# Causal mask of a chunked state-space scan: from mask matmuls to a GpSimd select

## What is computed

```python
def step(state, inp):
    x_t, b_t, c_t, dt_t = inp
    decay = jnp.exp(dt_t * a)[..., None, None]      # a < 0, 8 heads
    b_bar = dt_t[..., None] * b_t
    state = decay * state + b_bar[..., None] * x_t[:, :, None, :]
    y_t = jnp.einsum('bhn,bhnp->bhp', c_t, state)
    return (state, y_t)
```

## Time and profile before

| | |
|---|---|
| median of 3 runs | 1684.99 us (1682.63 to 1688.21) |
| the profiled execution's own time | 1682.11 us |
| its span in the trace | 1680.3 us |
| mean granted TensorE clock | 0.941 of full |
| TensorE busy | 1496.8 us, 89% |
| VectorE busy | 1211.4 us, 72% |
| ScalarE busy | 662.6 us, 39% |
| GpSimd busy | 473.3 us, 28% |

### The profile page before, as it was taken

The page is one execution under the profiler, slowest core; times in us unless marked ns, Lnnn a source line. Parts: engine busy times, 40 slices in busy tenths (PEclk is TensorE's granted clock), DMA queues, the critical chain, the costliest instruction groups (busy, mean ns, idle before and its releaser), DMA issues.

```text
span 1680.3 us, 22635 instructions
## 1 busy us (share of the span) xinstructions
PE 1496.8 (89%) x8504; PEld 924.9 (55%) x8504; DVE 1211.4 (72%) x2746; ACT 662.6 (39%) x1193; POOL 473.3 (28%) x496
## 2 busy tenths in 40 slices
PE   7989979998999979999899989999899998997445
PEld 2436635665456645666356654666456663565334
DVE  1357897489775897578974897858974789747861
ACT  4451434533263332714346332643337143551012
POOL 3003431336103341043313261043410443122610
PEclk9999999999999989999899989999899998999756
DMA  7000010011002010020100110020100201001100
GB/s 270 1 0 26 7 44 16 15 53 44 22 1 67 1 50 17 1 67 7 44 17 10 58 45 22 1 67 7 44 16 1 67 7 44 16 5 38 44 22 4
DMA packets 47309, 54.25 MB, mean 32 GB/s; under 512 B 7384, under 2 KB 42072, under 8 KB 47200
## 3 DMA queue, kind: packets, MB, share of 16 engines
q1 hardware_dynamic: 41184, 46.45, 8.4%
q0 software_dynamic: 6016, 6.35, 1.4%
HBM read 34.86 MB, written 17.87 MB: 31 GB/s over the span
## 4 chain that ended last, share of the span: by engine, by line
PE 38%; issue 27%; DVE 20%; POOL 9%; ACT 3%; DMA 2%; DVEq 0%; POOLq 0%
PE ps L1450 18%; PE ps L1602 7%; DVE xT L951 5%; POOL EC L519 4%; DVE Mt L1182 3%; PE ps L1515 2%; PE ps L1509 2%; DMA Mt<-mask,midx 2%; PE ps L1554 1%; POOL out L594 1%; ACT BT L637 1%; DVE st L889 1%; DVE EC L1173 1%; PE ps L1635 1%; PE ps L1438 1%
## 5 line engine op out<-in xcount | busy, mean ns | idle before, releaser
L1450 PE MATMUL ps<-xT,wb_s 128*128 128x512 f32 x512 | 232.0, 600 | 8.9 <-ACT xT L676 8.9
L1450 PE MATMUL ps<-xT,wc_s 128*128 128x512 f32 x512 | 237.7, 615 | 0.0
L726 ACT ACTIVATE Eg<-ps 128x512 f32<-128x512 f32 x128 | 76.4, 597 | 295.8 <-DVE Mt L1046 219.7
L951 DVE SCALAR_TENSOR_TENSOR xT<-xc,cols_s,xT 128x512 f32<-128x512 f32 x192 | 162.5, 892 | 3.2 <-ACT xT L669 0.6
L1450 PEld LDWEIGHTS ps<-xT,wc_s 128*128 128x128 f32 x512 | 99.4, 198 | 115.3 <-issue 114.9
L1450 PEld LDWEIGHTS ps<-xT,wb_s 128*128 128x128 f32 x512 | 94.3, 191 | 119.5 <-issue 103.9
L1450 PE MATMUL ps<-hT,wz_s 128*128 128x512 f32 x256 | 122.4, 635 | 0.0
L1602 PE MATMUL ps<-CT,xT 128*128 128x256 f32 x512 | 113.3, 382 | 7.7 <-DVE xT L1134 7.7
L587 POOL TENSOR_TENSOR sm<-sm,mhalf 128x1 f32<-128x1 f32 x24 | 14.5, 604 | 374.5 <-DVE sm L1337 345.0
L1450 PE MATMUL ps<-hT,wx_s 128*128 128x512 f32 x256 | 114.7, 603 | 0.9 <-ACT hT L648 0.9
L1602 PEld LDWEIGHTS ps<-CT,xT 128*128 128x128 f32 x512 | 98.2, 192 | 24.3 <-issue 11.1
(11 more groups left out here) (286 smaller groups left out, 3017.8 us busy)
## 6 DMA issues: line engine op xcount, KB each, us to landing
BT<-x SPq DMA_DIRECT2D x8, 1024.0 KB, 5.4
xr<-x SPq DMA_DIRECT2D x8, 1024.0 KB, 7.2
x_scratch<-xr SPq DMA_DIRECT2D x32, 256.0 KB, 2.5
out<-EC SPq DMA_DIRECT2D x32, 256.0 KB, 2.2
modrow<-mod_scratch SPq DMA_DIRECT2D x8, 512.0 KB, 4.0
w_s<-w SPq DMA_DIRECT2D x2, 1024.0 KB, 11.7
xT<-wmod SPq DMA_DIRECT2D x1, 1024.0 KB, 8.7
wb_s<-wbT SPq DMA_DIRECT2D x1, 1024.0 KB, 11.1
```

The source lines that it names most:

```text
L726: a.activation(Eg[:, s * HALF:(s + 1) * HALF], ps[s][:, :], ACT.Exp).then_inc(Eg_ready, 1)
L951: ins = v.scalar_tensor_tensor(dst, xcv[:, m, half * HALF + tap:half * HALF + tap + HALF], cols_s[:, m, tap:tap + 1], dst, ALU.mult, ALU.add)
L1450: ins = t_.matmul(bank[:, :], w[:, k, m * P:(m + 1) * P], rhs[:, k, half * HALF:(half + 1) * HALF], start=k == 0, stop=k == nk - 1)
```

## The change

The two mask matmuls of a chunk go, and the tile `causal` with them. The decay difference is then not masked, and above the diagonal it is positive. So ScalarE makes two passes for each half: Relu of minus the difference from PSUM into `Eg`, which bounds the exponent at zero, then the exponential of minus that in place. GpSimd then sets the entries with t < s to zero, in place, with an affine select (`make_causal`), and VectorE's masked product waits for the select (`causal_ready`) instead of for the exponential. TensorE may refill ps0 and ps1 once Relu has read them (`fall_ready`).

GpSimd's order changes too. `carry` is split in two halves: half 0 (`dec` and four products) comes first, then the select of chunk 0; in the loop over chunks the select of chunk c comes first, then the state's decay, and behind chunk 1 the second half of `dec` with two products, behind chunk 2 the last two. `ln_in` of the next batch stays behind the loop, and so behind the select of chunk 7.

```diff
-            def carry(b):
-
-                pool.wait_ge(*proj.read(b, J_EC + 7))
-                g.tensor_tensor(dec[:, :, :], ECv[:, :, P - 1::P], ones4[:, :, :], ALU.mult).then_inc(dec_ready, 1)
-                pool.wait_ge(dec_ready, at(dec_ready, b, 1))
-                pool.wait_ge(*proj.read(b, J_BC[1][7]))
-                for half in range(2):
-                    for k in range(KC):
-                        s = ECv[:, k, half * HALF:(half + 1) * HALF]
-                        g.tensor_tensor(s, s, CT[:, half, k, :], ALU.mult).then_inc(CE_ready, 1)
+            def carry(b, half):
+
+                pool.wait_ge(*proj.read(b, J_EC + 4 * half + 3))
+                pool.wait_ge(*proj.read(b, J_BC[half][7]))
+                g.tensor_tensor(dec[:, :, 4 * half:4 * half + 4],
+                                ECv[:, :, half * HALF + P - 1:(half + 1) * HALF:P],
+                                ones4[:, :, 0:4], ALU.mult).then_inc(dec_ready, 1)
+                pool.wait_ge(dec_ready, at(dec_ready, b, half + 1))
+
+            def carry_columns(b, half, ks):
+
+                for k in ks:
+                    s = ECv[:, k, half * HALF:(half + 1) * HALF]
+                    g.tensor_tensor(s, s, CT[:, half, k, :], ALU.mult).then_inc(CE_ready, 1)
+
+            def make_causal(b, c):
+
+                for s in range(2):
+                    pool.wait_ge(Eg_ready, at(Eg_ready, b, 2 * c + s + 1))
+                    e = Eg[:, s * HALF:(s + 1) * HALF].rearrange("p (h n) -> p h n", h=4)
+                    g.affine_select(out=e, in_=e, compare_op=ALU.is_ge, fill=0.0, base=0,
+                                    pattern=[[0, 4], [1, P]], channel_multiplier=-1).then_inc(causal_ready, 1)
 
             def decays(b):
 
-                for c in range(1, T - 1):
-                    pool.wait_ge(S_ready, at(S_ready, b, c))
-                    g.tensor_tensor(Sdc[:, :, :], Sbd[:, :, :], dec[:, :, c:c + 1].broadcast_to([P, KC, P]),
-                                    ALU.mult).then_inc(Sdc_ready, 1)
+                make_causal(b, 0)
+                for c in range(1, T):
+                    make_causal(b, c)
+                    if c < T - 1:
+                        pool.wait_ge(S_ready, at(S_ready, b, c))
+                        g.tensor_tensor(Sdc[:, :, :], Sbd[:, :, :], dec[:, :, c:c + 1].broadcast_to([P, KC, P]),
+                                        ALU.mult).then_inc(Sdc_ready, 1)
+                    if c == 1:
+                        carry(b, 1)
+                    if c in (1, 2):
+                        carry_columns(b, 1, (2 * c - 2, 2 * c - 1))
...
             def rest(b, last=False):
-                carry(b)
+                carry(b, 0)
+                carry_columns(b, 0, range(KC))
                 decays(b)
...
-                for c in range(T):
+                def decay(c):
                     for s in range(2):
                         act.wait_ge(cd_filled, at(cd_filled, b, 2 * c + s + 1))
                         if c or later(b):
                             act.wait_ge(Mt_ready, at(Mt_ready, b, 2 * (c - 1) + s + 1 if c else 0))
-                        a.activation(Eg[:, s * HALF:(s + 1) * HALF], ps[s][:, :], ACT.Exp
-                                     ).then_inc(Eg_ready, 1)
+                        a.activation(Eg[:, s * HALF:(s + 1) * HALF], ps[s][:, :], ACT.Relu, scale=-1.0
+                                     ).then_inc(fall_ready, 1)
+                    for s in range(2):
+                        e = Eg[:, s * HALF:(s + 1) * HALF]
+                        act.wait_ge(fall_ready, at(fall_ready, b, 2 * c + s + 1))
+                        a.activation(e, e, ACT.Exp, scale=-1.0).then_inc(Eg_ready, 1)
...
-                        dve.wait_ge(Eg_ready, at(Eg_ready, b, 2 * c + s + 1))
+                        dve.wait_ge(causal_ready, at(causal_ready, b, 2 * c + s + 1))
...
-                            pe.wait_ge(Eg_ready, at(Eg_ready, b, 2 * (c - 1) + s + 1 if c else 0))
-                        t_.matmul(ps[s][:, :], identb[:, :], causal[:, :, :].rearrange("p a n -> p (a n)"),
-                                  start=True, stop=False)
+                            pe.wait_ge(fall_ready, at(fall_ready, b, 2 * (c - 1) + s + 1 if c else 0))
                         t_.matmul(ps[s][:, :], Lw[:, c * P:(c + 1) * P], R8[:, 4 * s:4 * s + 4, c * P:(c + 1) * P],
-                                  start=False, stop=True).then_inc(cd_filled, 1)
+                                  start=True, stop=True).then_inc(cd_filled, 1)
```

More of the change, by code:

```diff
@@ L44 @@
 SD_MOD, SD_MIX, SD_ALL = 10, 14, 18
-SP_ALL = 68
+SP_ALL = 66
 CHAINS = {"A": 2, "V": 9, "D": 14, "S": 3, "G": 17, "R": 33, "O": 8}
@@ L135, in adaln_block @@
         identb = sb("identb", [P, P], BF16)
-        causal = sb("causal", [P, 4, P], BF16)
         ones_b = sb("ones_b", [P, 1], BF16)
@@ L287, in adaln_block @@
         v_ready = sig("v_ready")
-        dec_ready = sig("dec_ready")
+        dec_ready = sig("dec_ready", 2)
         CE_ready = sig("CE_ready", 8)
+        causal_ready = sig("decay_made_causal", 2 * T)
+        fall_ready = sig("decay_exponent_bounded", 2 * T)
         cd_filled = sig("cumdiff_filled", 2 * T)
@@ L465, in _ @@
                                  base=0, pattern=[[1, P]], channel_multiplier=-1))
-            link(g.memset(causal[:, :, :], 0.0))
-            link(g.affine_select(out=causal[:, :, :], in_=causal[:, :, :], compare_op=ALU.is_ge, fill=MASKED,
-                                 base=0, pattern=[[0, 4], [1, P]], channel_multiplier=-1))
             link(g.memset(ones_b[:, :], 1.0))
@@ L725, in scan @@
                             act.wait_ge(Mt_ready, at(Mt_ready, b, 2 * (c - 1) + s + 1 if c else 0))
-                        a.activation(Eg[:, s * HALF:(s + 1) * HALF], ps[s][:, :], ACT.Exp
-                                     ).then_inc(Eg_ready, 1)
+                        a.activation(Eg[:, s * HALF:(s + 1) * HALF], ps[s][:, :], ACT.Relu, scale=-1.0
[4 more added lines that the diff above has]
+                        a.activation(e, e, ACT.Exp, scale=-1.0).then_inc(Eg_ready, 1)
+                for c in range(T):
+                    decay(c)
                 if not last:
```

## The result

The changed kernel takes 1741.13 us (median; 1736.04 to 1743.75) against 1684.38 us for the kernel before on the same chip: 1.0328 times as long, 95% interval 1.0307 to 1.0348. The forecast was 1757, range 1715 to 1785, slower. The profiled execution took 1741.05 us, with a span of 1739.2 us; before they were 1682.11 and 1680.3. So the span grew by 58.9 us.

What follows compares the result with a forecast made beforehand. TensorE was taken to bound only chunks 3 to 5 of a middle batch, VectorE and GpSimd's queue other places. Six middle batches at 11.1 us, plus 1.0 and 4.3, gave 72 on 1684.99: 1757, range 1715 to 1785.

Steps and rivals of the forecast that it cites:

- Front: Chunk 0's select queues behind scatter, `dec` and four products; state update of chunk 1 comes 2.8 us later, before clock effects.
- Chunk 2 to 3: TensorE has lost its lead, so this period takes 5.5 us in place of 4.5: 1.0 more.
- The loop: Chunks 3 to 5, TensorE's limit: two mask matmuls less take 6.02 us to 5.39; 1.3 us gained per middle batch.
- In chunk 5 to 7 VectorE is the limit and the gain is nothing: Late chunks of a middle batch's scan: removing the mask matmuls gains no time there.
- Tail: GpSimd selects chunk 7 before the next batch's norm factors: 3.9 us later, TensorE waiting 4.9 in place of 0.99.
- Hidden in the middle: Mid-scan, the Relu, Exp and select chain fits before the next masked product, with 1.1 us to spare for its first half.
- Both rivals on prices: Select at 1.235 us gives 1774 (12%); Relu and Exp needing different tables, 1.283 us a load, near 1805 (4%).
- Sum: Middle batch 11.1 us with the clock, batch 0 +1.0, batch 7 +4.3: 72 us in total.
- the clock's in the tail: TensorE at half speed after the idle time behind the scan: 2.1 us, bounds nothing and 2.6.
- the clock's in front: TensorE at half speed after 7.3 us idle at the scan's start: 2.6 us, bounds nothing and 2.6.
- three more periods: Batch 7 gains from the removed matmuls in three more periods, a term of -2.1 us in its +4.3.
- Faster: the front opens up: GpSimd's queue before chunk 0: an early select wins the whole 5.35 us wait for `Sdc`; -24 us, 1661 (4%).

Runs made afterwards that it cites:

- e13_warm_short: Changed kernel with 7 unread f32 matmuls of 128 rows in TensorE's idle time ahead of the output of chunk 0; 1722.67 us, 1.0217 times the kernel before.
- e2_front: Changed kernel with the select of chunk 0 put ahead of `dec` and the four products, still behind the scatter; 1697.75 us, 1.0084 times the kernel before.
- e4_split: Kernel before, masks by matmul, with only the products on `EC` split: four ahead of chunk 0, two each behind chunks 1 and 2; 1675.11 us, 0.995.
- e1_tail: Changed kernel with the next batch's norm factors put ahead of the select of chunk 7 on GpSimd; 1715.26 us, 1.0179 times the kernel before.
- e12_queue2: Changed kernel with the scatter right behind the select of chunk 0 and the next norm factors ahead of the select of chunk 7; 1649.31 us, 0.9781.
- e14_masks_same_order: Kernel before, mask matmuls kept, with products split four, two, two and the scatter right behind the first four; 1676.28 us, 0.9946 times the kernel before.
- e7_warm: Changed kernel with 30 unread bf16 matmuls of 48 rows in TensorE's idle time ahead of the output of chunk 0; 1741.14 us, 1.034.
- e9_queue: Changed kernel with six products before the select of chunk 0, scatter right behind it, two products behind chunk 1, norm factors before chunk 7's select; 1673.34 us, 0.994.

## Why the prediction was right, point by point

- *Front.* Right. The state update of chunk 1 came 5.0 us later, counted from the scatter's start (18.98 less the 14.02 of before, means of batches 1 to 6; in batch 3 it is 4.1); 2.8 and 2.6 of clock were forecast. In e13_warm_short, where the clock holds, it comes at 16.68, so the delay itself is 2.7 and the clock's share 2.3. The masked product of chunk 0 starts 8.57 behind the scatter; 8.67 was forecast (725.45 less 716.78). e2_front showed the place.
- *Chunk 2 to 3.* Right: +0.8, forecast +1.0. The prediction put 5.5 there, where its own loop of 5.39 gives +0.9. e4_split shows the same loss of lead without the select.
- *The loop.* Right where it was claimed: 5.38 in each of the two periods, forecast 5.39. **Wrong is "In chunk 5 to 7 VectorE is the limit and the gain is nothing"**, as a statement of cost. Chunk 5 to 6 keeps its 9.03, but chunk 6 to 7 takes 6.06 where it took 4.50: TensorE, through sooner, waits 1.41 and 1.10 us for VectorE, and from 778 on its granted clock is 0.50. In the changed kernel that is hidden, since the first transpose of the next batch waits for GpSimd's factors anyway. In e1_tail and e12_queue2 the stretch from chunk 6 stays 0.8 us above that of before; 0.6 of it is ScalarE's two more passes (see e1_tail), which the prediction's 3.9 us for the tail hold already, and only the 0.1 to 0.2 behind the first transpose can be the clock's. What the clock costs there when nothing hides it, one batch shows: in batch 5 of e14_masks_same_order the granted clock was 0.70 from 1144 to 1148, chunk 6 to 7 took 5.51 in place of 4.50, and the output projection came 0.5 us later than in the other middle batches of that kernel.
- *Tail.* The first transpose of the next batch starts 8.25 us behind the masked product of chunk 6, forecast 8.4. What follows it took 1.6 longer, forecast 2.1 of clock (a mean: nothing in batches 1 and 5, 1.6 to 2.7 in the other four). Together 5.3 for 6.0. The idle time itself was 2.38 in batch 3 and 2.1 to 3.4 in the others, not the 4.9 of the prediction, because TensorE's work ahead of it, from 778 on, ran at half clock.
- *Hidden in the middle.* Right: from chunk 4 on GpSimd waits 2.50 for ScalarE before the select, but for chunk 6 (0.18, behind another product), and VectorE waits for a select only 7 times, 52.0 us in all, each time at chunk 0. Both rivals on prices fall: 638 ns a select, and no table load among ScalarE's rows at lines 744 and 749.
- *Sum.* A middle batch: 5.0 + 0.8 - 1.3 + 5.3 = 9.8, forecast 11.1, batch 0 +0.3 for +1.0, batch 7 +3.0 for +4.3. 6 x 9.8 + 0.3 + 3.0 = 62 of the 72 forecast. **The mis-sized terms are the clock's in the tail (1.6 for 2.1), the clock's in front (2.3 for 2.6) and a tenth or two in the others.** The 2.1 that batch 7 gains doesn't follow from "three more periods"; measured are four of 0.64 in chunks 3 to 7, 2.6. And batches 1 to 6 don't all repeat batch 3 within 0.1 us: before, batch 6 takes 14.69 in chunks 0 to 2 where it takes 14.34. The span grew by 58.9, so 3 more came back outside the scan. The table has it as 205.5 - 196.2 = 9.3 per batch in place of 9.8. One place that I saw is the router's step behind 7 us of idling: in batches 3 to 6 the low clock behind it lasts 6.8 us in place of 10.2. Why was not tried.
- *"Faster: the front opens up"* had the right place, but not the price. As the change stands it didn't happen. e12_queue2 brings it about by hand, and that its 1649 lies near the 1661 given there is in part luck: up to chunk 6 it gains 4.5 us a batch where the rival took 5.35 + 1.3, and its tail, mended too, costs 0.8 in place of 3.9.

## What to carry to other kernels

An operation moved to another engine goes into that engine's order, and its place there counts for more than its price: the same 128 selects of 0.64 us made this kernel 3.3% slower or 2.2% faster. Work out for the first and the last use when the input is ready, what stands ahead in the queue then, and who waits behind; put the new step ahead of what nobody needs yet, but ask what a moved transfer in turn holds up. Count an idle gap on TensorE together with the slow stretch behind it: here 2.3 to 2.6 us on top of a gap of 7.

## What was not expected of the hardware

- A stream without a gap didn't hold TensorE's clock. With 30 bf16 matmuls of 48 rows back to back the granted clock went from 1.00 to 0.81 and then 0.50; with 7 f32 matmuls of 128 rows (14 records) in the same place it stayed at 1.00. The Trainium skill, "TensorE: Matmul & The Clock Gate", section "What's actually happening", ties the clock to how busy the engine has recently been. By e7_warm, busy in the trace's sense is not enough. Type, rows and weights differ between the two fills, so which of them counts stays open.
- Two short waits, 1.41 and 1.10 us, in a stretch in which TensorE was busy for 1.49 of 4 us were followed by a clock of 0.50. In the kernel before, TensorE was busier in the same chunk, the mask matmuls among its work, and kept 1.00:

```profile
753.00:757.00 4.00, 3.07 (x28) 1.73 (x24) 3.92 (x18) 0.00 (x0) 0.00 (x0) 1.00 0.00 0
757.00:761.00 4.00, 3.28 (x46) 2.81 (x48) 3.27 (x9) 1.67 (x3) 3.10 (x4) 1.00 0.00 0
```

That it was busier can't be the whole of it: in batch 5 of e14_masks_same_order TensorE was busy for 3.23 us of 1140 to 1144, and the granted clock of the next 4 us was 0.70.

- The same wait of 2.51 us (e9_queue) was followed by the lower clock in five batches and by the full one in two.
- A matmul behind one with the same weights cost 0.215 us in the loop, one between matmuls with other weights 0.315.
- A VectorE step with two SBUF inputs took 1.38 us in place of 0.48 beside GpSimd's products, and a masked product with one input in PSUM lost nothing beside them.
